# First stage of a fused gated cross-attention kernel: an eighth of every fourth tanh computed through exp on GpSimd and VectorE, and a quarter of the additions on GpSimd

## What is computed

```
txt_proj  = textual_features @ Ws                  # 64 rows of 512 per batch
feat_proj = layernorm(x) @ W                       # 1024 rows of 512 per batch
h   = tanh(txt_proj[:, None] + feat_proj[:, :, None] + b)   # 1024 x 64 x 512 per batch
rho = einsum('bftd,d->bft', h, w)
att = softmax(rho masked by q_masks)
w_s, b_s = tanh(att @ txt @ Wcw + bcw), tanh(att @ txt @ Wcb + bcb)
x = x + tanh(g) * (w_s * layernorm(x) + b_s)
```

## Time and profile before

| | us |
|---|---|
| median of 3 runs | 1926.75 (1923.69 to 1926.92) |
| the profiled execution | 1925.59 |
| its span, first to last instruction | 1923.5 |
| busy PE / DVE / ACT / POOL | 1577.8 / 1713.1 / 1476.9 / 613.9 |

### The profile page before, as it was taken

One profiled execution on the slowest core, in us unless ns is written; L12 is line 12 of the kernel. 1 busy time (PEld: TensorE's weight loads), 2 busy tenths in 40 slices (PEclk: granted clock), 3 DMA queues, 4 the chain that ended last, 5 costly groups with the idle time before them and its releaser, 6 DMA issues.

```text
span 1923.5 us, 24394 instructions
## 1 busy us (share of the span) xinstructions
PE 1577.8 (82%) x9406; PEld 708.5 (37%) x9473; DVE 1713.1 (89%) x2626; ACT 1476.9 (77%) x1091; POOL 613.9 (32%) x482
## 2 busy tenths in 40 slices
PE   7778965688556975786489978999999987899996
PEld 4232211122111321232134435666666653444442
DVE  6999999999999998889689977899999867999997
ACT  4899999999999999999745755445554436888881
POOL 1000000000000000000044236666666643999991
PEclk9999999999999999999989989999999999999999
DMA  5000200010000010000079884333333111122212
GB/s 205 2 7 19 85 12 1 22 65 30 6 1 0 18 36 25 1 1 12 0 249 395 289 243 138 102 112 110 115 102 109 44 55 39 44 78 77 66 55 77
DMA packets 123269, 146.54 MB, mean 76 GB/s; under 512 B 31374, under 2 KB 80654, under 8 KB 122770
## 3 DMA queue, kind: packets, MB, share of 16 engines
q1 hardware_dynamic: 123154, 144.98, 23.0%
HBM read 87.55 MB, written 51.77 MB: 72 GB/s over the span
## 4 chain that ended last, share of the span: by engine, by line
ACT 44%; PE 30%; DVE 14%; issue 4%; POOL 4%; DMA 3%; SPq 1%; DVEq 0%; ACTq 0%; POOLq 0%
ACT unit L557 41%; PE psum L1762 5%; PE psum L1796 5%; PE psum L1058 4%; PE psum L1748 3%; DVE unit L463 2%; POOL h L1937 2%; PE psum L1772 2%; PE psum L1789 2%; PE psum L1819 2%; DVE psum L1528 1%; DVE psum L1533 1%; POOL hidden L1954 1%; PE psum L1781 1%; PE psum L609 1%
## 5 line engine op out<-in xcount | busy, mean ns | idle before, releaser
L557 ACT ACTIVATE unit<-unit 128x4096 f32<-128x4096 f32 x244 | 857.4, 3606 | 0.5 <-DVE unit L463 0.3
L463 DVE TENSOR_SCALAR unit<-feat_proj,text_proj 128x1024 f32<-128x1024 f32 x976 | 667.5, 746 | 64.4 <-PE psum L697 61.5
L697 PE MATMUL psum<-unit,w_pad 128*32 128x512 f32 x3904 | 470.4, 600 | 227.9 <-ACT unit L557 227.7
L697 PEld LDWEIGHTS psum<-unit,w_pad 128*32 128x32 f32 x3904 | 102.0, 109 | 543.2 <-ACT unit L557 386.9
L744 POOL TENSOR_SCALAR red<-red 128x8 f32<-128x8 f32 x4 | 2.0, 508 | 531.5 <-DVE red L338 531.5
L1819 PE MATMUL psum<-xq_block,w_q 128*128 128x512 bf16 x489 | 119.9, 385 | 15.7 <-ACT h L1695 11.2
L1937 POOL TENSOR_TENSOR h<-h,arow 128x512 f32<-128x512 f32 x104 | 125.6, 1231 | 20.0 <-ACT h L1695 20.0
L744 POOL TENSOR_SCALAR rstd<-mv 128x8 f32<-128x8 f32 (+1 forms) x5 | 1.7, 335 | 406.1 <-DVE mv L233 406.1
L609 PE MATMUL psum<-xnT,W_sb 128*128 128x512 f32 x256 | 125.5, 619 | 1.9 <-ACT xnT L511 1.9
L1670 ACT ACTIVATE scores<-scores 128x1024 f32<-128x1024 f32 x32 | 33.9, 1058 | 114.0 <-POOL scores L1923 114.0
L1954 POOL TENSOR_TENSOR hidden<-hidden,srow 128x2048 f32<-128x2048 f32 x28 | 114.4, 4084 | 10.1 <-DVE hidden_q L1563 9.7
(11 more groups left out here) (260 smaller groups left out, 2695.7 us busy)
## 6 DMA issues: line engine op xcount, KB each, us to landing
h_scratch<-h SPq DMA_DIRECT2D x44, 512.0 KB, 6.1
hin<-h_scratch SPq DMA_DIRECT2D x32, 704.0 KB, 4.6
xin<-in_x SPq DMA_DIRECT2D x8, 1024.0 KB, 5.6
tern_in<-in_w1T SPq DMA_DIRECT2D x16, 512.0 KB, 6.0
tern_in<-in_w2T SPq DMA_DIRECT2D x16, 512.0 KB, 6.9
x<-in_x SPq DMA_DIRECT2D x16, 512.0 KB, 3.7
x_scratch<-x SPq DMA_DIRECT2D x32, 256.0 KB, 2.0
x3in<-x_scratch SPq DMA_DIRECT2D x31, 256.0 KB, 3.2
```

The lines of the kernel that those rows point to most:

```text
L463: ins = ve.tensor_scalar(units[:, n % 3, k, :], FP[:, bi % 2, k, :], TP[:, k, n:n + 1], None, ALU.add)
L557: ac.activation(units[:, n % 3], units[:, n % 3], ACT.Tanh).then_inc(unit_tanh, 1)
L697: mm = te.matmul(psum[k * TG:(k + 1) * TG, 3 + 2 * grp + half, :], w_pad[:, k, TG - 1 - tt:2 * TG - 1 - tt], units[:, n % 3, k, half * BAN ...
```

## The change

**Light units.** 48 of the 244 units, those with t % 4 = 1 in a part of each group (`LIGHT`: 9, 13, 13 and 13 in the four batches), leave out the tanh of chunk 3's second half. The ACT instruction covers 128x3584 elements for them. For the half left out, tanh(a) = 1 - 2 / (1 + exp(2a)) is formed so:

- Once for each batch, exp(2a) is split for the features and for the text rows into a power of two and a mantissa: GpSimd finds the exponents (`split`), DVE the remainders (`remainder`, 4 scalar_tensor_tensor), ACT the exp of them (`mantissas`, 128x512 and 128x64).
- For each light unit GpSimd adds the exponents as integers, multiplies by the features' mantissa, multiplies by the text's and adds 1 (`light_denominator`, three instructions of 128x512).
- DVE takes the reciprocal in two pieces of 128x256, behind the additions of the second and third unit after it (`reciprocals`).
- PE adds it with weights -2w into the unit's row by one more matmul behind the fourth unit after it, and the constants w of a group by one more matmul each (`light_sum`).

**Additions.** Chunk 0 of every unit is added by GpSimd, and chunk 1 too in the second and third unit after a light one (`pool_chunks`). 340 additions of 128x1024 move to GpSimd. DVE keeps 3, 2, 2 or, in the light unit, two and a half. ACT waits for both engines.

**Around it.** The mask is added by PE, as a first matmul into the PSUM bank of rho (`rho_mask`). One of the two products per batch goes to GpSimd (`products`). For the last accumulator of all, the first half is copied by DVE as soon as its matmuls are done, and the second by ACT. The roots of GpSimd get fixed places in its loop.

```diff
-    prod = sb("prod", [P, TPB, TXT], stack=pa)
+    prod = sb("prod", [P, 2, TPB, TXT], stack=pa)
     red = sb("red", [P, 12, TPB], stack=pa)
...
     TAIL_END = 50
+    MASK_AT = 32
+    LIGHT_FIRST, LIGHT_END, LIGHT_EVERY = 1, (28, 24), 4
+    LIGHT = [bi * TXT + grp * TG + tt for bi in range(NB) for grp in range(2)
+             for tt in range(LIGHT_FIRST + (16 if bi + grp == 0 else 0), LIGHT_END[grp], LIGHT_EVERY)]
+    REC_AFTER, SUM_AFTER = (2, 3), 4
+    CONST_AT = 2
+    SPLIT_AT, REST_AT = 60, (62, 63)
...
+    def pool_chunks(n):
+        return 2 if any(n - d in LIGHT for d in REC_AFTER) else 1
+
+    def light_half(n):
+        return 1 if n in LIGHT else 2
...
+        def reciprocals(n):
+            for part, after in enumerate(REC_AFTER):
+                if n - after in LIGHT:
+                    j = LIGHT.index(n - after)
+                    piece = light[:, j % 2, part * (BANK // 2):(part + 1) * (BANK // 2)]
+                    V.wait_ge(light_step, light_count(n - after) + 3)
+                    ve.reciprocal(piece, piece).then_inc(light_vec, 1)
...
+        for step in range(2):
+            remainder(0, step)
...
-            for k in range(KC):
-                ins = ve.tensor_scalar(units[:, n % 3, k, :], FP[:, bi % 2, k, :], TP[:, k, n:n + 1], None, ALU.add)
+            for k in range(pool_chunks(n), KC):
+                part = slice(0, BANK * (light_half(n) if k == KC - 1 else 2))
+                ins = ve.tensor_scalar(units[:, n % 3, k, part], FP[:, bi % 2, k, part], TP[:, k, n:n + 1], None, ALU.add)
             ins.then_inc(unit_added, 1)
+            reciprocals(n)
+            if t in REST_AT and bi + 1 < NB:
+                remainder(bi + 1, REST_AT.index(t))
...
+        def mantissas(bi):
+            A.wait_ge(light_vec, rest_count(bi) + 4)
+            for m in (feat_mant, text_mant):
+                ac.activation(m[:, :], m[:, :], ACT.Exp, scale=2.0).then_inc(mant_done, 1)
...
-            ac.activation(units[:, n % 3], units[:, n % 3], ACT.Tanh).then_inc(unit_tanh, 1)
+            A.wait_ge(pool_added, POOL_ADDED0 + n + 1 - RAMP)
+            unit = units[:, n % 3].rearrange("p k s -> p (k s)")[:, 0:(2 * KC - 2 + light_half(n)) * BANK]
+            ac.activation(unit, unit, ACT.Tanh).then_inc(unit_tanh, 1)
+            if n == RAMP:
+                mantissas(0)
+            if t == TXT - 1 and bi + 1 < NB:
+                mantissas(bi + 1)
+        A.wait_ge(unit_mm, NU - RAMP)
+        A.wait_ge(sel_mm, 4 * NB - 2)
+        ac.activation(RP[:, 1, :], psum[:, 6, :], ACT.Copy).then_inc(ramp_tanh, 1)
         for s in range(TAIL_END):
             tail(NB - 1, s)
...
-                mm = te.matmul(psum[:, 7, c0:c0 + TG], RP[:, r % 2, f * P:(f + 1) * P], sel[:, :], start=True, stop=True)
+                mm = te.matmul(psum[:, 7, c0:c0 + TG], RP[:, r % 2, f * P:(f + 1) * P], sel[:, :], start=False,
+                               stop=(grp == 1 and half == 1 and f == TPK - 1))
...
+            if n - SUM_AFTER in LIGHT:
+                j = LIGHT.index(n - SUM_AFTER)
+                at = (n - SUM_AFTER) % TG
+                T.wait_ge(light_vec, reciprocal_count(n - SUM_AFTER) + 2)
+                te.matmul(psum[strip, 4 + 2 * grp, :], w_neg[:, TG - 1 - at:2 * TG - 1 - at], light[:, j % 2, :],
+                          start=False, stop=False, tile_position=(0, (KC - 1) * TG)).then_inc(light_mm, 1)
...
-                for k in range(KC):
+                for k in range(KC - half * (2 - light_half(n))):
                     mm = te.matmul(psum[k * TG:(k + 1) * TG, 3 + 2 * grp + half, :],
                                    w_pad[:, k, TG - 1 - tt:2 * TG - 1 - tt],
                                    units[:, n % 3, k, half * BANK:(half + 1) * BANK],
                                    start=(tt == 0), stop=(tt == TG - 1), tile_position=(0, k * TG))
+                if n == NU - 1 and half == 0:
+                    mm.then_inc(ramp_mm, 1)
             mm.then_inc(unit_mm, 1)
+            light_sum(n)
+            if t == MASK_AT:
+                rho_mask(bi)
...
+        def light_denominator(n):
+            bi, t = divmod(n, TXT)
+            j = LIGHT.index(n)
+            den = light[:, j % 2, :]
+            G.wait_ge(light_mm, j - 1)
+            done = light_count(n)
+            G.wait_ge(light_step, split_count(bi) + 5)
+            gp.tensor_scalar(den.bitcast(U32), feat_exp[:, :], text_exp[:, 1, t:t + 1], TOP, ALU.add,
+                             ALU.min).then_inc(light_step, 1)
+            G.wait_ge(mant_done, MANT0 + 2 * bi + 2)
+            G.wait_ge(light_step, done + 1)
+            gp.tensor_tensor(den, den, feat_mant[:, :], ALU.mult).then_inc(light_step, 1)
+            G.wait_ge(light_step, done + 2)
+            gp.tensor_scalar(den, den, text_mant[:, t:t + 1], 1.0, ALU.mult, ALU.add).then_inc(light_step, 1)
...
+            G.wait_ge(unit_mm, n - 2 - RAMP)
+            G.wait_ge(text_copied, KC if bi == 0 else 2 * KC)
+            if n < RAMP + 3:
+                G.wait_ge(ramp_mm, 2 * (RAMP - SLOTS // 2 + n - RAMP + 1))
+            for k in range(pool_chunks(n)):
+                add = gp.tensor_scalar(units[:, n % 3, k, :], FP[:, bi % 2, k, :], TP[:, k, n:n + 1], None, ALU.add)
+            add.then_inc(pool_added, 1)
+            if n in LIGHT:
+                light_denominator(n)
+            if t == 10 and 0 < bi < NB - 1:
+                moments_root(bi + 1)
+            if t == 20 and bi > 0:
+                products(bi - 1)
```

More of the change, by code:

```diff
@@ L20 @@
 MAGIC = 1.5 * 2.0 ** 23
+EXPONENT = 2.0 ** 23
+BIAS = 127.0
+OCTAVES = 2.8853900817779268
+HALF_LN2 = 2839.0 / 8192.0
+HALF_LN2_REST = 0.34657359027997264 - 2839.0 / 8192.0
+TOP = 253.0 * 2.0 ** 23
 INV127 = 1.0 / QMAX
@@ L283, in rho_copy @@
             r = 4 * bi + 2 * grp + half
[L284 removed]
+            if r == 4 * NB - 2:
+                V.wait_ge(ramp_mm, HALF_SUMMED)
+            else:
+                V.wait_ge(unit_mm, bi * TXT + (grp + 1) * TG - RAMP)
             V.wait_ge(sel_mm, r - 1)
@@ L651, in ramp_rho, with light_sum @@
             mm.then_inc(ramp_mm, 1)
+        def light_sum(n):
+            bi, t = divmod(n, TXT)
+            grp, tt = divmod(t, TG)
+            strip = slice((KC - 1) * TG, KC * TG)
+            if tt == CONST_AT or n == RAMP:
+                T.wait_ge(start_step, 3)
+                te.matmul(psum[strip, 4 + 2 * grp, :], w_light[:, 0 if bi + grp == 0 else 2 - grp, :],
+                          ones[:, 0:1].broadcast_to([P, BANK]), start=False, stop=False,
+                          tile_position=(0, (KC - 1) * TG))
+            if n - SUM_AFTER in LIGHT:
[4 more added lines that the diff above has]
+                          start=False, stop=False, tile_position=(0, (KC - 1) * TG)).then_inc(light_mm, 1)
         def keys(m, k0, k1):
@@ new lines, in moments_root, with split @@
+        def moments_root(bi):
+            t0 = bi * TPB
+            G.wait_ge(mv0_done, t0 + TPB)
+            root(mv[:, t0:t0 + TPB, 1], rstd0[:, t0:t0 + TPB], TPB, rstd0_done, TPB)
+        def split(bi):
+            cols = slice(bi * TXT, (bi + 1) * TXT)
+            raw, biased = text_exp[:, 0, :], text_exp[:, 1, :]
+            G.wait_ge(fp_copied, (bi + 1) * 2 * KC)
+            G.wait_ge(text_copied, KC if bi == 0 else 2 * KC)
+            for exp, val in ((feat_exp[:, :], FP[:, bi % 2, KC - 1, BANK:2 * BANK]), (raw, TP[:, KC - 1, cols])):
+                gp.tensor_scalar(exp, val, OCTAVES, MAGIC, ALU.mult, ALU.add).then_inc(light_step, 1)
+            G.wait_ge(light_step, split_count(bi) + 2)
+            gp.tensor_scalar(feat_exp[:, :], feat_exp[:, :], MAGIC, EXPONENT, ALU.subtract,
+                             ALU.mult).then_inc(light_step, 1)
+            gp.tensor_scalar(biased, raw, MAGIC - BIAS, EXPONENT, ALU.subtract, ALU.mult).then_inc(light_step, 1)
+            G.wait_ge(light_step, split_count(bi) + 4)
+            gp.tensor_scalar(raw, raw, MAGIC, EXPONENT, ALU.subtract, ALU.mult).then_inc(light_step, 1)
```

128 lines of the change are left out of this document (94 added, 34 removed).

## The result

The changed kernel takes 2433.98 us (median of 4 runs, 2430.09 to 2438.30), the kernel before 1925.22 us beside it. The ratio is 1.2645 (95% interval 1.2629 to 1.2661): 508 us slower, where 1917.5 us and a range up to 1950 had been forecast.

What follows compares the result with a forecast made beforehand. ACT was taken to bound the first stage without a gap; -20.4 + 3.7 - 2.1 + 5.6 + 3.9 = -9.3 us from 1925.6 gave 1916.3, and 1.2 us to the median made 1917.5 us, range 1904 to 1950.

Steps and rivals of the forecast that it cites:

- ACT's saving: In the light units' tanh on ACT: 512 fewer elements save 0.426 us each, 20.4 us for 48 units.
- all fits: Rival for the first stage: three tiles hide the waits, PE's busy time overstates; -18.8 us, 1908 us, chance 0.16.
- GpSimd's price for an addition: GpSimd's 128x1024 additions in the first stage: 1.3 us each, 7.8 us for a group's six.
- GpSimd itself is the bound: Rival: in the first stage GpSimd's additions take 2.6 us, a group some 20 us; +280 us, chance 0.03.
- The sum of exponents: GpSimd's step in light units: among the 512-column instructions said to hold DVE's additions off 0.45 us each.
- DVE held off: DVE's additions beside GpSimd: 7.4 us held per group, 2.0, 1.7, 3.3 delaying additions; hand-overs return 0.5 to 0.9.
- GpSimd's additions fall on DVE's: Main rival: in batches 0 to 2, 0.9 us more per group meets DVE's additions; +22.2 us, 1949 us, chance 0.31.
- DVE's own work: DVE in a group, waits aside: 12.4, 12.6 and 10.7 us in three stretches, under 13.63; 256-element reciprocal 1.68 us.
- PE in the middle stretch: Batches 0 to 2, t = 41 to 53: added matmuls bring PE to 56.6 us, costing 12 groups 5.6 us.
- The end: End of the first stage: copies split, mask on PE, a product on GpSimd; 0.7 us each, 2.1 us gained.
- The port rule: DVE and GpSimd share ports: instructions exclude each other, the later standing still throughout, so their additions can't overlap.

Runs made afterwards that it cites:

- pool_tiny: all_two_op with every GpSimd addition and the three light-unit instructions cut to 16 columns, for measuring only: 1907.93 us, 0.991.
- forms: The kernel before with ten forms of GpSimd instruction on a 128x1024 scratch tile, four of each, put into GpSimd's idle time: 1961.46 us.
- add_two_op: The changed kernel with GpSimd's 340 additions alone written as times 1.0 plus the scalar: 2042.47 us, 1.0602.
- all_two_op: add_two_op with the exponents' sum and the split also as multiply and add, exponents clamped once per batch: 2029.66 us, 1.0547.
- adds_only_two_op: The changed kernel without light units, each unit having one multiply-and-add addition on GpSimd and three additions on DVE: 1928.29 us, 1.0022.

## Why the prediction was wrong

- **ACT's saving, 20.4 us:** right. A light tanh took 3.18 us. With everything else short (pool_tiny) the kernel was 16.3 us faster, where the case "all fits" had 18.8.
- **GpSimd's price for an addition, 1.3 us:** this step failed. The prediction had two rows for it. The durations of 334 ns for 11 columns and 597 for 128 said 2.6 us for 1024, and it priced that case with some 2200 us and gave it 0.03. It was talked away by one row, in which a delayed instruction ended 0.13 us after DVE. That instruction was one with a single operation, and what it had not yet done at DVE's end says nothing of its length: as the forms show, a slow instruction and DVE go on side by side. The other row, 1.04 us for 1024 columns, was a min and a max, another form. The measured addition is 2.88 us without DVE's and 3.24 beside them. This step is 391.5 us, by add_two_op. With it, the forecast that GpSimd's 11 us for a group lie under ACT's 13.63 fell: they were 23.9. The rival "GpSimd itself is the bound" had the right path, and was still some 230 us short, mostly since it took 2.6 us for an addition where 3.24 were measured.
- **The sum of exponents, 0.45 us of holding and 0.9 in all:** wrong for the same reason, 2.23 us. With the split it is 12.8 us.
- **DVE held off, 1.4, 1.1 and 2.5 us a group in the end:** the mechanism was right, the size not. From pool_tiny to all_two_op DVE's busy time with whole additions grew from 419.1 to 599.8 us and with the halves from 23.1 to 47.9, 205 us together; in the groups with a light unit it is 3.4 to 3.5 us each in batches 0 to 2 and 4.0 in batch 3. The prediction had 2.0, 1.7 and 3.3 us there, and took off 0.5 to 0.9 for hand-overs. That what lies beside reciprocals is free held: they take 1.74 us in both runs. But the additions of DVE were delayed by 0.7 to 1.8 us a group more than had been allowed before the hand-overs. This is the main rival's mechanism, "GpSimd's additions fall on DVE's". It was priced with one instruction a group more, and with the terms of the forecast it came to +22 us; with the fast forms it measured +104.
- **DVE's own work:** right. The reciprocal of 256 columns took 1.74 us, where 1.68 was estimated from 16 columns. With GpSimd's instructions short (pool_tiny), ACT waited 0.9 us for DVE in all.
- **PE in the middle stretch, 5.6 us:** wrong. With the added matmuls its busy time is 52.4 of 56 us in pool_tiny, where 56.6 was forecast and 52.7 stood before, and ACT has no gap there. So the added matmuls didn't cost there what a lone matmul's row gave; why is open.
- **The end, 2.1 us:** seen in the profile, 2.2 us, but not in the median.
- **The port rule:** The Trainium skill ("SBUF — State Buffer", Who interferes with whom) has the later of the two instructions stand still for the whole of the other. The slow forms do not fit with it: four additions of DVE of 0.68 us and one GpSimd instruction of 2.84 us at least are 5.6 us one after the other, and ended within 4.4. The fast forms don't contradict it: in adds_only_two_op each GpSimd addition, 1.11 us at least, took 0.45 us more than that, and DVE's busy time grew by 0.7 us for each of them. That one stands still for the whole of the other is not shown by these sums.

## What to carry to other kernels

The price of an instruction on GpSimd belongs to its form: take it from a row with the same pair of operations, not only with the same shape. Write a single add or multiplication of fp32 on GpSimd as multiply and add; here that alone was 391 us. And count what GpSimd's instructions cost DVE: here each fast addition moved to GpSimd lengthened DVE's others by 0.7 us, as much as one addition of its own. Last, an average over a stretch in which one engine has room says little of a stretch in which it has less, or of single units.

## What was not expected of the hardware

- tensor_scalar on GpSimd, 128x1024 fp32, least of four: one operation 3.14 to 3.32 us, add and min 3.92, subtract and mult 3.95, mult and add 1.41, min and max 1.08. A tensor_tensor add, 2.21 us, is faster than adding a constant with one operation.
- A slow GpSimd instruction slows DVE's additions to 1.1 us each (four in 4.37 us, in forms) but does not stop them.
- The mean granted clock of TensorE, which has the two levels of 1.2 and 2.4 GHz, was 0.985 of full speed before and 0.871 in the changed kernel, though PE did nearly the same work. PE had long gaps there: 518.8 us of idle time ahead of the units' matmuls, against 227.9 before, and a record of these matmuls has 797 ns on average, against 600.
